# The product with V of the second attention is copied from PSUM by VectorE and not by ScalarE

## The reference, cut to what matters

```python
q = rms_norm(x, qn_scale) @ q_w.T + q_b      # 16 heads of 8 features; k the same
v = x @ v_w.T + v_b
q, k = apply_rotary(q, cos, sin), apply_rotary(k, cos, sin)
scores = jnp.einsum('bhqd,bhkd->bhqk', q, k) * scale
weights = jax.nn.sigmoid(scores)
weights = weights / (jnp.sum(weights, axis=-1, keepdims=True) + EPS_RENORM)
attn = jnp.einsum('bhqk,bhkd->bhqd', weights, v)
out = attn.transpose(0, 2, 1, 3).reshape(B, L, D) @ o_w.T + o_b
x = layernorm(x + out)
```

## Time and profile before

| | us |
|---|---|
| median of 3 runs | 1220.67 |
| the profiled execution, whole | 1220.22 |
| its span, first to last instruction | 1217.7 |
| TensorE busy (PE) | 1087.3 |
| VectorE busy (DVE) | 877.4 |
| ScalarE busy (ACT) | 760.1 |
| GpSimd busy (POOL) | 426.6 |

### The profile page before, as it was taken

The page is one execution under the profiler, slowest core; times in us unless marked ns, Lnnn a source line. Parts: engine busy times, 40 slices in busy tenths (PEclk is TensorE's granted clock), DMA queues, the critical chain, the costliest instruction groups (busy, mean ns, idle before and its releaser), DMA issues. The chain is left out here.

```text
span 1217.7 us, 20906 instructions
## 1 busy us (share of the span) xinstructions
PE 1087.3 (89%) x6064; PEld 507.4 (42%) x6064; DVE 877.4 (72%) x2074; ACT 760.1 (62%) x969; POOL 426.6 (35%) x434
## 2 busy tenths in 40 slices
PE   3999999999999865999999999947999999999695
PEld 1122222222222254777777777723333333322473
DVE  4879999999999368898889888667445444422387
ACT  1067777777777952455545555415888888899352
POOL 0312322413410153556556655523232233300264
PEclk9999999999999976999999999968999999999898
DMA  5452222222120000000000000005312332110001
GB/s 161 132 204 71 79 60 91 74 62 91 53 74 2 2 1 0 1 1 0 0 0 0 0 0 1 1 26 175 115 60 61 103 103 91 61 56 1 1 26 43
DMA packets 53465, 63.43 MB, mean 52 GB/s; under 512 B 8636, under 2 KB 38204, under 8 KB 53020
## 3 DMA queue, kind: packets, MB, share of 16 engines
q1 hardware_dynamic: 53416, 62.83, 16.4%
HBM read 35.15 MB, written 27.26 MB: 51 GB/s over the span
## 5 line engine op out<-in xcount | busy, mean ns | idle before, releaser
L560 DVE TENSOR_REDUCE a_nmax<-a_ps_f 128x1 f32<-128x512 f32 x512 | 322.4, 684 | 41.3 <-PE a_ps_f L428 37.8
L373 ACT ACTIVATE a_prob<-a_ps_s 128x1024 f32<-128x1024 f32 x256 | 252.5, 1025 | 76.8 <-PE a_ps_s L488 75.1
L766 ACT ACTIVATE a_prob<-a_ps_s 128x1024 f32<-128x1024 f32 x256 | 248.6, 1033 | 61.6 <-PE a_ps_s L821 58.9
L1560 POOL TENSOR_TENSOR moe_hl<-moe_hid,moe_hh 128x512 fp32r<-128x512 f32 x136 | 179.2, 1318 | 146.4 <-ACT moe_hh L1483 145.7
L428 PE MATMUL a_ps_f<-a_ks,a_qs 48*128 48x512 bf16 x512 | 176.7, 413 | 29.0 <-DMA a_ks<-parts_k 10.6
L834 PE MATMUL a_ps_o<-a_prob,a_va 128*32 128x512 f32 x1024 | 136.4, 605 | 2.5 <-ACT a_osb L754 1.3
L501 PE MATMUL a_ps_o<-a_prob,a_va 128*32 128x512 f32 x1024 | 138.0, 612 | 0.3
L488 PE MATMUL a_ps_s<-a_qs,a_ks 51*128 51x512 bf16 x512 | 135.0, 387 | 3.2 <-ACT a_prob L373 2.8
L1477 ACT ACTIVATE moe_gated<-moe_ps 128x512 f32<-128x512 f32 x136 | 81.1, 596 | 90.5 <-PE moe_ps L1405 90.4
L428 PEld LDWEIGHTS a_ps_f<-a_ks,a_qs 48*128 48x128 bf16 x512 | 40.2, 94 | 231.5 <-DVE a_nmax L560 190.8
L1483 ACT ACTIVATE moe_hh<-moe_hid 128x512 fp32r<-128x512 f32 x136 | 85.7, 630 | 67.6 <-DVE moe_hid L1515 66.5
(11 more groups left out here) (210 smaller groups left out, 1612.1 us busy)
## 6 DMA issues: line engine op xcount, KB each, us to landing
parts_q<-a_parts SPq DMA_DIRECT2D x48, 256.0 KB, 2.5
parts_k<-a_parts SPq DMA_DIRECT2D x48, 256.0 KB, 2.5
a_qs<-parts_q SPq DMA_DIRECT2D x128, 96.0 KB, 2.3
a_ks<-parts_k SPq DMA_DIRECT2D x128, 96.0 KB, 2.4
a_xt<-in_x_t SPq DMA_DIRECT2D x8, 256.0 KB, 3.0
out_x<-g_X SPq DMA_DIRECT2D x8, 256.0 KB, 2.3
moe_wg<-in_wg SPq DMA_DIRECT2D x1, 1088.0 KB, 5.7
moe_wu<-in_wu SPq DMA_DIRECT2D x1, 1088.0 KB, 7.9
```

Of the source, the lines that this page charges most:

```text
L373: nc.scalar.activation(prob[:, u % PSLOTS, :, :], ps_s[:, u % 2, :, :], ACT.Exp, scale=float(P) ** -0.5).then_inc(exp_done, 1)
L560: nc.vector.tensor_reduce(nmax[:, half_no, h % 2, col:col + 1], ps_f[:, bank, :], AX.X, ALU.max, negate=True).then_inc(max_done, 1)
L766: nc.scalar.activation(prob[:, u % PSLOTS, :, :], ps_s[:, u % 2, :, :], ACT.Sigmoid, scale=float(HD) ** -0.5).then_inc(exp_done, 1)
L1560: nc.gpsimd.tensor_tensor(hl[:, part_at(j), :], hid[:, hid_at(j), :], hh[:, part_at(j), :], ALU.subtract).then_inc(hl_done, 1)
```

## The change

The copy `take_o` leaves the list of ScalarE and enters that of VectorE, at the same units, with the same waits. On VectorE it stands behind `take_v` when both are due and ahead of `divide`. Nothing else changes.

```diff
         @block.scalar
...
-            def take_o(b, grp):
-                act.wait_ge(ot_done, NG * b + grp - 1 + OT_C)
-                take(osb[:, grp % 2, :], ps_o[:, :], pv_done, NE * b + NT * (grp + 1) + PV_C, o_taken)
-
             def units(b, p, u0, u1, qk_on, front, back, tail):
...
-                    if u % 8 == 1 and (back if u > 8 else tail):
-                        take_o(*((b, u // 8 - 1) if u > 8 else (b - 1, NG - 1)))
 
             act.sem_inc(exp_done, EXP_C)
-            act.sem_inc(o_taken, O_C)
             walk(act, units, LOOP_U1, True)
-            take_o(NB - 1, NG - 1)
...
         @block.vector
...
+            dve.sem_inc(o_taken, O_C)
...
+            def take_o(b, grp):
+                dve.wait_ge(ot_done, NG * b + grp - 1 + OT_C)
+                dve.wait_ge(pv_done, NE * b + NT * (grp + 1) + PV_C)
+                nc.vector.tensor_copy(osb[:, grp % 2, :], ps_o[:, :]).then_inc(o_taken, 1)
+
...
                     if front and u == V1_AT:
                         take_v(b + 1, 1 - p)
+                    if u % 8 == 1 and (back if u > 8 else tail):
+                        take_o(*((b, u // 8 - 1) if u > 8 else (b - 1, NG - 1)))
                     if u % 8 == TURN_AT and (back if u > 8 else tail):
                         divide(*((b, u // 8 - 1) if u > 8 else (b - 1, NG - 1)))
...
             walk(dve, units, LOOP_U1, True)
+            take_o(NB - 1, NG - 1)
             divide(NB - 1, NG - 1)
```

More of the change, by code:

```diff
@@ L751, in _ @@
         def _(act):
-            def take(dst, src, ready, value, done):
-                act.wait_ge(ready, value)
-                nc.scalar.activation(dst, src, ACT.Copy).then_inc(done, 1)
-            def take_o(b, grp):
-                act.wait_ge(ot_done, NG * b + grp - 1 + OT_C)
-                take(osb[:, grp % 2, :], ps_o[:, :], pv_done, NE * b + NT * (grp + 1) + PV_C, o_taken)
             def units(b, p, u0, u1, qk_on, front, back, tail):
```

## The result

The changed kernel takes 1240.25 us (median of 4, 1238.27 to 1243.55), the kernel before 1219.51 in the same runs. The ratio is 1.0171, 95% interval 1.0157 to 1.0186: 20.9 us more, where 18.9 was forecast. The profiled execution has a span of 1239.4 against 1217.7, so the two traces account for 21.7.

The account below looks back on a forecast made before the run. TensorE's own sequence was taken as the bound, with ScalarE close behind. Batches 1 to 5 12.5, batch 0 3.7, batches 6 and 7 1.8 and clock 0.9 sum to 18.9; 1220.2 + 18.9 = 1239.1 us, range 1229 to 1247.

Parts of the forecast that it names:

- The step that carries the forecast: In a steady batch VectorE reaches the copies of groups 0 and 1 late, so TensorE stalls twice: +2.5 per batch.
- Theory 2: Rival in the follow-up experiments: a copy by VectorE costs something wherever it stands, 0.65 us each; no chance given.
- Copy of group 0: Unit 9: the copy waits behind add_x and the layernorm statistics on VectorE, so pv(4) starts 1.63 us later.
- Copy of group 1: Unit 17: the copy waits behind part_x and rms on VectorE; pv(8) starts 2.93 us later, 1.47 of it new.
- The give-back behind it: After pv(8): TensorE's former 0.58 wait for a_xr absorbs delay, leaving 2.28, then 2.5 us with the late rest.
- Groups 2 and 3: Units 25 and 1: other TensorE work between the two pv gives the copy about 1.5 us; cost 0.
- Batch 0: Unit 9 of the first batch: the copy comes behind weight preparation and taking V of batch 1; +3.7 us.
- Batches 6 and 7: Last two batches: unit 9 stalls cost 3.0, later copies off ScalarE give back 1.2; +1.8 us.
- the relief of ScalarE: Batches 6 and 7 from unit 16: sigmoids need not step aside for copies; gains 0.64 and 0.55 us.
- The clock: Batch 0's 3.7 us idle TensorE may halve its clock, costing about 1.7 or 0; the middle, +0.9, was taken.
- signs of being wrong: Profile signs: a batch under 39 us, a copy within 0.1 of pv's end, or granted clock below 1.00 between 850 and 1140.
- the 1259: Rival, chance 0.07: the clock falls in every stall, twelve of 1.5 to 1.8 us, about 1.7 each; +20, 1259 us.

Follow-up runs that it names:

- the doubled copies: The changed kernel with VectorE's copies of groups 2 and 3 made twice, first into a buffer nobody reads: 1244.58 us, ratio 1.0197.

## Why the prediction was right

**The bound, and the cost by place.** The step that carries the forecast holds: both stalls are where the prediction put them, released by VectorE's copy, with the instruction in front that it named. Theory 2 is out: 16 copies cost 0 in one kernel and 3.2 us as additions in another, 8 cost 14, and one alone cost 4.4.

**Copy of group 0.** Forecast +1.63 at pv(4), measured 2.21 - 0.71 = 1.50. The prediction let the copy start behind the end of the last statistics instruction at full length. It starts 0.09 before that end (968.04 against 968.13) and takes 0.66: what has no dependence on VectorE overlaps a little. At the end of the batch it is worth 1.32.

**Copy of group 1.** pv(8) was forecast 2.93 later, measured (978.62 - 966.55) - (966.56 - 957.27) = 2.78; the difference is the one above. The give-back behind it was forecast to leave 2.5 and left 2.2. In batch 2, where the clock holds, the s2 behind the xr transposes begins 1.03 after the first block of transposes, while the sum had 1.18: here two blocks back to back took less than twice one. The wait for the rest a_xrl was 0.2, as forecast.

**Groups 2 and 3** cost nothing, as said, and their slack is real (the doubled copies).

**Batch 0.** 3.4 for 3.7. The copy began right behind take_v, 3.56 after pv(3).

**Batches 6 and 7.** 1.9 for 1.8, but by two wrong sizes that cancel. In the kernel with group 0 alone on VectorE the two batches take 2.4 more (34.76 and 25.03), where the stalls were to cost 3.0. The other copies gain 0.6 (0.4 with group 1 alone, 0.2 with groups 2 and 3 alone), where the relief of ScalarE was to give 1.2. That relief alone is not worth a measurable time (ratio 1.0003).

**The clock** is the term that was mis-sized: 0.9, a mean of 0 and 1.7 for one fall in batch 0. It was 4.5, three falls of some 1.5. The price of a fall was right (1.7 said, 1.48 measured in batches 3 and 5); their number was wrong. Batch 0's fall was taken as a matter of one in two and came in every trace that has the stall unfilled. One of the prediction's own signs of being wrong also came, a granted clock below 1.00 between 850 and 1140; it was too strict, since the sum itself counted half a fall in batch 0. The prediction had falls behind the shorter stalls as a rival, in all twelve of them, at 0.07. What happened lies between, two of twelve in this trace and four of five in the kernel with group 1's copy alone. The Trainium skill (TensorE: Matmul & The Clock Gate, section A second HAM failure mode: psum-queue depth-cycling) describes a kernel whose clock went back and forth over TensorE's short idle times. This trace agrees in part: both falls in batches 1 to 7 came behind 1.38 us of idle time, and ten stalls of 1.38 to 1.67 us had none, so the 1259 did not come.

The steady batches were over-sized by 1.4 us and the clock under-sized by 3.6. That 1239.1 came so near 1240.25 is in part luck, since these two errors work against each other. Of the smaller signs, ScalarE's idle time per batch grew by 3.9 us (busy 31.36 of 40.21, before 33.12 of 38.05), not by 5.

**What stays open.** Which of the stalls is followed by a fall. Over the nine traces that have unfilled stalls of 1.4 to 2.3 us in batches 1 to 7, it was 21 of 79: in one kernel four of the five of group 1, in another none of the same five, in others those of group 0. Batch 1 is 0.24 longer than the other undisturbed ones (885.89 to 926.34), in several kernels. About 1 us behind the stage comes from a clock at half for 16.9 us in place of 10.2 where the last block begins; the kernel that copies groups 2 and 3 alone has no stall and shows 17 us there too, with 89.6 us behind its last pv in place of 88.9, so no stall is needed for it. It loses nothing by all its runs, so this 1 us may be scatter between executions.

## What to carry to other kernels

An engine with half its time free may still be the wrong home for a short instruction on the path: ask what stands in front of it in that engine's written order at the moment its input is ready, not how busy the engine is. Replay one period from start to start, with the give-back behind each stall (what the bound engine would have waited for anyway). And count each new idle stretch of TensorE of the lengths seen here twice, once for itself and once for the chance that the clock falls behind it.

## What the runs showed that was not expected

The clock fell behind some idle stretches of 1.4 to 1.7 us, which stood alone in otherwise full work, and behind none of the waits of 1.05 us that the kernels with the copy inside rms have; each fall lasted about 3.4 us in batches 3 and 5 of the changed kernel and cost 1.5. Filling the idle time with unread matmuls kept the clock at 1.00 and made the kernel faster with more work in it (1237.81 against 1240.25). Two independent copies on VectorE start 0.58 to 0.61 apart though each is listed with 0.66 to 0.69, so the list of durations overstates a row of independent ones by some 0.1 each.
